# Attention probabilities of the first head turned by DMA and VectorE instead of TensorE

## The chip, the core and the metric

The kernel runs on one core of a Trainium2 chip. The metric is the device time of one launch, in microseconds. An execution of it is compared with executions of the kernel before on the same chip.

## What is computed

Sixteen sequences (B = 16) of 512 tokens with 512 features pass through three layers: linear attention with a small convolution (phase a), cross attention on a second sequence (phase b, which the change touches), and a gated recurrence over the sequences with an output layer (phases c and d). Cut to phase b, the reference is:

```python
NUM_HEADS, NUM_KV, HEAD_DIM, WIDTH = (4, 1, 128, 512)
xn = _rmsnorm(x, rms_scale)
mn = _rmsnorm(mem_seq, rms_scale)
q = jnp.einsum('BTD,NDH->BTNH', xn, q_w)
kv = jnp.einsum('BSD,cKDH->cBSKH', mn, kv_w)
k, v = (kv[0], kv[1])
q = _apply_rope(q, q_pos) * HEAD_DIM ** (-0.5)
k = _apply_rope(k, k_pos)
logits = jnp.einsum('BTKGH,BSKH->BKGTS', q, k, preferred_element_type=jnp.float32)
masked = jnp.where(mem_mask[:, None, None, None, :], logits, MASK_FILL)
probs = jax.nn.softmax(masked, axis=-1).astype(x.dtype)
enc = jnp.einsum('BKGTS,BSKH->BTKGH', probs, v).reshape(B, T, NUM_HEADS, HEAD_DIM)
return jnp.einsum('BTNH,NHD->BTD', enc, out_w)
```

## The kernel before

Every matrix is held as a high and a low part (`Split`), and `product` (L128 to L132) multiplies with three matmuls, high by high, high by low, low by high. Phase b is a software pipeline over the sequences (`pipeline3`): in one step the sequence `new` is prepared (keys, values, queries), `old` goes through the softmax, and `fin` gets its last encodings, the output product and the residual. There are 18 steps. A step has 16 slots (`j` from 0 to 15); each engine runs its own program, written by hand as a loop over the slots, strictly in that order. There is no scheduler: what an engine does in a slot is what the `if` lines say.

The softmax of one sequence has 16 tiles of 128 queries by 512 keys, four per head; tiles 0 to 3 are head 0. A tile passes through: `logits` on TensorE (two slots ahead of its own); `masked` on VectorE (L1531: mask, minimum and copy to one of four places of `soft`); `exp` on ScalarE (L1379); `one_over` on VectorE (L1520); `normalise` on GpSimd (L1316); `turn_p` on TensorE (L1723: four 128x128 transposes into PSUM, at the end of its slot); `p_high` on ScalarE (L1388) and `p_low` on VectorE (L1539), which split the turned tile. `masked` of a tile waits until `turn_p` has read the tile four before it in `soft`. `encode` multiplies the four turned tiles of a head with the values: head 0 in slot 8, head 1 in slot 11, head 2 in slots 13 to 15, head 3 in slot 1 of the next step.

In the same slots `new` is worked on. Its normalised tokens `x` are turned without TensorE: SyncE stores them to DRAM (`out` is used as scratch, L1118), loads them back with 32-row blocks exchanged (`load_shuffled`, L382, four DMAs), and VectorE transposes 32x32 squares within partitions (`tokens_turned`, L388, slots 5 to 8). ScalarE splits the result (`tokens_high`, slots 5 to 8, each ahead of that slot's `exp`), GpSimd makes the low part (`tokens_low`, L1320), and TensorE takes it in `queries(0)` in slot 9. `residual` (VectorE, slots 5 to 8) empties the banks of `out`, the output product of `fin` (TensorE, slots 4 to 7); `out`, keys, queries and `turn_keys` share three PSUM banks in turn, so that `out(3)` takes the bank that `residual(0)` has emptied and `turn_keys` the one of `residual(1)`.

All DMAs are issued by SyncE, one after the other, and SyncE stands still at each wait. Before, its order in a step is: load `res`; wait for the normalised tokens and store them; wait for the store and issue the four shuffled loads; load the mask, the next memory (L1109) and the next tokens; store the finished sequence.

## Time and profile before

| | |
|---|---|
| median of 3 runs | 3030.55 us (3030.36 to 5046.9) |
| profiled execution | 3028.35 us, of which the span of the instructions is 3026.6 us |
| TensorE busy | 2983.4 us (99%), 14628 matmuls |
| VectorE, ScalarE, GpSimd busy | 1952.0 us (64%), 1295.3 us (43%), 919.5 us (30%) |
| mean granted TensorE clock | 0.997 of full speed |
| the probabilities' transposes (L1723) | 1024, busy 154.5 us |
| one step of phase b | 57.3 us, from the token store at 1452.44 us to the next at 1509.66 us |

The time of an execution is 1.75 us more than its span, and the sums below are made against the profiled execution. A matmul's row overlaps the next one's, so that what a group costs TensorE is read from start to start. In the timelines a number in brackets is the idle time ahead of a row and what ended it.

### The profile page before, as it was taken

The page shows a single profiled execution, that of the slowest core. Times are in us where ns is not written, and L with a number is a line of the kernel's source. Part 1 is how long each engine was busy: PE and PEld are TensorE (multiplying, and loading weights), DVE is VectorE, ACT ScalarE, POOL GpSimd, SP SyncE. Part 2 cuts the span into 40 slices and gives each one's busy share as a digit, 9 for nine tenths or more (in the row PEclk, how much of TensorE's full clock was granted, in tenths as well). Part 3 has the DMA queues.
Part 4 walks back from the last instruction along what each step waited for, and adds up shares of the span by engine and source line. Part 5 has one row for each costly group of instructions (what it writes and reads, how often), then busy time and mean ns, then how long its engine had stood idle before and what let it go on. Part 6 is the DMA issues. An engine that isn't in the chain of part 4 may idle for free.

```text
span 3026.6 us, 39400 instructions
## 1 busy us (share of the span) xinstructions
PE 2983.4 (99%) x14628; PEld 2508.4 (83%) x14628; DVE 1952.0 (64%) x4095; ACT 1295.3 (43%) x2511; POOL 919.5 (30%) x681
## 2 busy tenths in 40 slices
PE   7999999999989999999999999999999999999999
PEld 6888888888868888888888878888888888888887
DVE  6888888888878888888888774323333433232455
ACT  4444444444457766767766643211112212112243
POOL 0101010101357877777777720000000000000144
PEclk9999999999999999999999999999999999999999
DMA  7777777777733334344344232111111121111486
GB/s 212 201 203 209 202 215 199 215 198 217 205 105 113 105 107 127 99 113 127 99 114 126 71 125 74 56 54 55 42 42 42 56 55 57 42 28 46 153 290 224
DMA packets 319631, 380.07 MB, mean 126 GB/s; under 512 B 15312, under 2 KB 175056, under 8 KB 319440
## 3 DMA queue, kind: packets, MB, share of 16 engines
q1 hardware_dynamic: 319440, 377.56, 43.2%
q8 instruction: 116, 1.90, 0.3%
q14 instruction: 75, 0.61, 0.1%
HBM read 232.80 MB, written 130.02 MB: 120 GB/s over the span
## 4 chain that ended last, share of the span: by engine, by line
PE 96%; DVE 2%; ACT 1%; issue 1%; DMA 0%; POOL 0%; SPq 0%; DVEq 0%; ACTq 0%; POOLq 0%
PE c_p L132 11%; PE c_p L131 11%; PE c_p L130 11%; PE a_p L130 6%; PE a_p L131 6%; PE a_p L132 6%; PE b_n L130 5%; PE b_n L132 5%; PE b_n L131 5%; PE b_t L1723 3%; PE d_p L131 2%; PE d_p L132 2%; PE d_p L130 2%; PE a_p L1017 2%; PE a_r L131 2%; PE a_r L132 2%
## 5 line engine op out<-in xcount | busy, mean ns | idle before, releaser
L1316 POOL TENSOR_SCALAR b_soft<-b_soft,b_one_in_sum 128x512 f32<-128x512 f32 x256 | 401.2, 1568 | 201.5 <-DVE b_one_in_sum L1520 201.3
L1997 ACT ACTIVATE c_gate<-c_p,c_bias 128x512 f32<-128x512 f32 x180 | 124.2, 690 | 682.6 <-PE c_p L132 682.6
L2027 DVE TENSOR_TENSOR c_gate<-c_gate,c_gate 128x512 f32<-128x512 f32 x64 | 44.2, 691 | 502.7 <-ACT c_gate L1997 502.7
L351 POOL TENSOR_TENSOR kept_scale<-c_ln_ve,minus_half 128x4 f32<-128x4 f32 x16 | 16.1, 1008 | 880.4 <-DVE c_ln_ve L343 880.4
L1531 DVE CUSTOM_DVE_ANT_0 b_soft<-b_l,b_mask_row 128x512 f32<-128x512 f32 x256 | 175.6, 686 | 87.9 <-issue 84.0
L351 POOL TENSOR_TENSOR a_ln_sc<-a_ln_ve,minus_half 128x4 f32<-128x4 f32 x16 | 16.3, 1017 | 629.9 <-DVE a_ln_ve L343 629.9
L1379 ACT ACTIVATE b_soft<-b_soft,b_minus_top 128x512 f32<-128x512 f32 x256 | 184.5, 721 | 44.6 <-DVE b_minus_top L1531 42.6
L649 ACT ACTIVATE a_elu<-a_p 128x512 f32<-128x512 f32 x128 | 75.6, 591 | 287.6 <-PE a_p L132 287.6
L1388 ACT ACTIVATE b_p_hi<-b_t 128x512 fp32r<-128x512 f32 x256 | 151.3, 591 | 109.9 <-PE b_t L1723 109.6
L1539 DVE TENSOR_TENSOR b_p_lo<-b_t,b_p_hi 128x512 fp32r<-128x512 f32 x256 | 175.7, 686 | 16.1 <-ACT b_p_hi L1388 14.3
L1723 PE MATMUL b_t<-ident,b_soft 128*128 128x128 f32 x1024 | 154.5, 273 | 4.9 <-POOL b_soft L1316 4.9
L2221 POOL TENSOR_TENSOR d_x<-d_x,d_y 128x512 f32<-128x512 f32 x60 | 79.8, 1332 | 252.8 <-ACT d_y L2238 252.8
L1723 PEld LDWEIGHTS b_t<-ident,b_soft 128*128 128x128 f32 x1024 | 126.0, 142 | 30.5 <-DVE b_p_lo L1539 6.4
L130 PE MATMUL b_l<-b_k_hi,b_q_hi 128*128 128x512 f32 x256 | 123.2, 481 | 2.0 <-POOL b_q_lo L1328 1.6
L2029 DVE TENSOR_TENSOR c_gate<-c_gate,c_c_f 128x512 f32<-128x512 f32 x64 | 44.3, 692 | 116.3 <-ACT c_gate L1997 116.3
L130 PE MATMUL a_p<-a_Wk_hi,a_xT_hi 128*128 128x512 f32 x256 | 105.3, 411 | 0.7 <-DVE a_Wk_lo L194 0.7
L626 POOL TENSOR_TENSOR a_res<-a_res,a_bp 128x512 f32<-128x512 f32 x64 | 82.3, 1318 | 75.9 <-DMA a_res<-in_x 47.4
L666 ACT ACTIVATE a_z_hi<-a_z_sum 128x512 fp32r<-128x512 f32 x64 | 40.5, 633 | 150.2 <-DVE a_z_sum L848 150.2
L130 PE MATMUL b_n<-b_nT_hi,b_qw_hi 128*128 128x512 f32 x256 | 100.7, 393 | 3.0 <-POOL b_nT_lo L1320 3.0
L130 PE MATMUL b_e<-b_p_hi,b_v_hi 128*128 128x512 f32 x256 | 100.4, 392 | 2.9 <-DVE b_enc_lo L1544 2.9
L132 PE MATMUL b_l<-b_k_hi,b_q_lo 128*128 128x512 f32 x256 | 102.0, 398 | 0.0
L130 PE MATMUL a_r<-a_Wp_hi,a_z_hi 128*128 128x512 f32 x256 | 101.2, 395 | 0.0
(301 smaller groups left out, 9617.6 us busy)
## 6 DMA issues: line engine op xcount, KB each, us to landing
a_mem_moving<-in_ctx SPq DMA_DIRECT2D x64, 256.0 KB, 5.2
a_mem_turned<-in_ctx SPq DMA_DIRECT2D x16, 1024.0 KB, 9.2
x<-a_mem_turned SPq DMA_DIRECT2D x16, 1024.0 KB, 7.8
a_res<-in_x SPq DMA_DIRECT2D x16, 1024.0 KB, 6.4
x<-a_res SPq DMA_DIRECT2D x16, 1024.0 KB, 5.2
b_memT_f<-x SPq DMA_DIRECT2D x16, 1024.0 KB, 7.3
b_x<-x SPq DMA_DIRECT2D x16, 1024.0 KB, 6.1
b_res<-x SPq DMA_DIRECT2D x16, 1024.0 KB, 5.5
```

Of the source, the lines that this page charges most:

```text
L130: pe.matmul(out, stationary.high, moving.high, start=first, stop=False)
L131: pe.matmul(out, stationary.high, moving.low, start=False, stop=False)
L132: return pe.matmul(out, stationary.low, moving.high, start=False, stop=last)
L626: pool.tensor_tensor(res[:, t, :], res[:, t, :], bp[:, :], ALU.add).then_inc(res_bp.sem, res_bp.unit)
L1316: pool.tensor_scalar(soft[:, at, :], soft[:, at, :], one_in_sum[:, at:at + 1], None, ALU.mult).then_inc(p_norm.sem, p_norm.unit)
L1379: act.activation(soft[:, at, :], soft[:, at, :], ACT.Exp, bias=minus_top[:, at:at + 1], scale=-1.0, accum_out=row_sum[:, at:at + 1]).then_ ...
L1388: act.activation(p[h % 2].high[:, :, t * P:(t + 1) * P], pT_banks[j % 2][:, :].rearrange("p (i s) -> p i s", i=T), ACT.Copy).then_inc(p_hi ...
L1531: dve.tensor_tensor_reduce(out=soft[:, at, :], in0=logit_banks[j % 2][:, :], in1=mask_row[b % 2][:, :], scale=-1.0, scalar=3e38, op0=ALU.a ...
L1539: dve.tensor_tensor(part.low, pT_banks[j % 2][:, :].rearrange("p (i s) -> p i s", i=T), part.high_f32(), ALU.subtract).then_inc(p_lo.sem, ...
L1723: mm = pe.transpose(pT_banks[j % 2][:, i * P:(i + 1) * P], soft[:, tile(old.b, j), i * P:(i + 1) * P], self.ident[:, :])
L1997: act.activation(gate[j % 2][i][:, :], gating.banks[(3 * j + i) % 6][:, :], ACT.Tanh if g == "c" else ACT.Sigmoid, bias=added[:, i, j:j + ...
L2221: pool.tensor_tensor(x[old.par][:, t, :], x[old.par][:, t, :], y[:, t % 2, :], ALU.add).then_inc(out_sb.sem, out_sb.unit)
```

## The change

In phase b the four tiles of head 0 are no longer turned by TensorE. For each, SyncE stores the normalised tile to DRAM (`store_p`, rows of `out`); for each half of two tiles it loads the blocks back exchanged, four DMAs of 64 KB for a tile (`load_p`, eight for a half), into the half of the second probability buffer that is free at that time, each tile with a place of its own (`shuffled_p`); VectorE transposes 32x32 squares (`first_head_turned`, slots 3 to 6); ScalarE and GpSimd split (`first_head_high`, `first_head_low`, slots 4 to 7). `load_p` of the second half also waits for the loads of the first. The place in `soft` of tiles 0 to 3 comes free when their stores have landed, in pairs (`soft_free`, `k | 1`). A square transpose yields columns that are interleaved by four, so the columns of keys and mask are written in that order (`by_column`, `by_tile`), and `turn_p` of heads 1 to 3 reads its columns with a step of four. Some semaphores are merged (`kvq_ps`, `k_mask`), with the same waits.

```diff
         SLOTS = 4
+        HEAD = 4
         with ExitStack() as held:
...
             q = self.split(ctx, "b_q", [P, H, S])
+            p0_at = self.place.offset
             p = [self.split(ctx, f"b_p{i}", [P, T, S]) for i in range(2)]
+            p0_raw = Place(nc, p0_at + 4 * T * S).tile("b_p0_raw", [P, T, S])
+            p1_raw = [Place(nc, p0_at + 4 * T * S * (2 + i)).tile(f"b_p1_raw{i}", [P, T, S]) for i in range(2)]
             memT = Split(sb("memT_hi", [P, C, S], F32R), Place(nc, self.base + 1024 * 196).tile("b_memT_lo", [P, C, S], F32R))
             memT_f = Place(nc, self.base + 1024 * 196).tile("b_memT_f", [P, C, S])
             rope = sb("rope", [P, 4, S])
...
-            def shuffle_x(sp, b):
+            def store_p(sp, b, t):
+                sp.wait_ge(p_norm.sem, p_norm.upto(b, t))
+                sp.dma_start(self.out[b, t * P:(t + 1) * P, :], soft[:, t, :]).then_inc(p_stored.sem, p_stored.unit)
+
+            def load_p(sp, b, half):
+
+                sp.wait_ge(p_stored.sem, p_stored.upto(b, 2 * half + 1))
+                if half == 1:
+                    sp.wait_ge(p_loaded.sem, p_loaded.upto(b, 7))
+                if half == 0 and b >= 1:
+                    sp.wait_ge(enc_ps.sem, enc_ps.upto(b - 1))
+                for i in range(2):
+                    t = 2 * half + i
+                    for a in range(4):
+                        sp.dma_start(shuffled_p(t)[32 * a:32 * (a + 1), :, :],
+                                     self.out[b, t * P:(t + 1) * P, a * P:(a + 1) * P].rearrange("(g m) n -> m g n", m=32)).then_inc(p_loaded.sem, p_loaded.unit)
+
+            def shuffled_p(t):
+                return p1_raw[t // 2][:, :, (2 + t % 2) * P:(3 + t % 2) * P]
+
+            def store_x(sp, b):
                 sp.wait_ge(N.normed.sem, N.normed.upto(b))
                 sp.dma_start(self.token_rows(self.out, b), x[:, :, :]).then_inc(x_moved.sem, x_moved.unit)
+
+            def shuffle_x(sp, b):
                 sp.wait_ge(x_moved.sem, x_moved.upto(b - 1, 0))
                 self.load_shuffled(sp, x, self.out, b, x_moved)
...
+            def by_tile(row):
+                return row[:, :].rearrange("p (i w) -> p w i", i=T)
+
+            def by_column(row):
+                return row[:, :].rearrange("p (w i) -> p w i", i=T)
+
+            def soft_free(b, j):
+
+                g = b * J + j - SLOTS
+                if g < 0:
+                    return None
+                item, k = divmod(g, J)
+                if k < T:
+                    return p_stored.sem, p_stored.upto(item, k | 1)
+                return pT_ps.sem, pT_ps.upto(item, k - T)
+
...
                             sp.wait_ge(self.a_stored.sem, self.a_stored.upto(B - 1))
                         sp.dma_start(res[:, :, :], self.token_rows(self.x1, fin.b)).then_inc(res_in.sem, res_in.unit)
+                    if old:
+                        store_p(sp, old.b, 0)
+                    if new and new.b >= 1:
+                        store_x(sp, new.b)
+                    if old:
+                        store_p(sp, old.b, 1)
+                        load_p(sp, old.b, 0)
                     if new and new.b >= 1:
                         shuffle_x(sp, new.b)
+                    if old:
+                        store_p(sp, old.b, 2)
+                        store_p(sp, old.b, 3)
+                        load_p(sp, old.b, 1)
                     if following(new, B):
...
+                    def first_head_low(t):
+                        pool.wait_ge(p_hi.sem, p_hi.upto(old.b, high_at[t]))
+                        part = (slice(None), slice(None), slice(t * P, (t + 1) * P))
+                        pool.tensor_tensor(p[0].low[part], p0_raw[part], p[0].high[part].bitcast(F32), ALU.subtract).then_inc(p0_lo.sem, p0_lo.unit)
+
...
-                        act.wait_ge(pT_ps.sem, pT_ps.upto(b, j))
+                        act.wait_ge(pT_ps.sem, pT_ps.upto(b, j - T))
+                        if j == T + 2:
+                            act.wait_ge(p_lo.sem, p_lo.upto(b, first_turned_at[T - 1]))
...
+                    def first_head_high(t):
+                        act.wait_ge(p_lo.sem, p_lo.upto(old.b, first_turned_at[t]))
+                        part = (slice(None), slice(None), slice(t * P, (t + 1) * P))
+                        act.activation(p[0].high[part], p0_raw[part], ACT.Copy).then_inc(p_hi.sem, p_hi.unit)
...
-                        act.activation(k[new.par].high[:, :], turns.bank(s, KT)[:, :], ACT.Copy).then_inc(k_hi.sem, k_hi.unit)
+                        act.activation(by_column(k[new.par].high), by_tile(turns.bank(s, KT)), ACT.Copy).then_inc(k_hi.sem, k_hi.unit)
...
-                        if old and j >= 1:
+                        if old and j >= T + 1:
                             p_high(old.b, j - 1)
+                        if old and HEAD <= j < HEAD + T:
+                            first_head_high(j - HEAD)
...
-                        if free := earlier(pT_ps, b, j, SLOTS):
+                        if free := soft_free(b, j):
...
+                    def first_head_turned(t):
+                        dve.wait_ge(p_loaded.sem, p_loaded.upto(old.b, 8 * (t // 2) + 7))
+                        if t == 0 and old.b >= 1:
+                            dve.wait_ge(enc_ps.sem, enc_ps.upto(old.b - 1, 2))
+                        blocks = shuffled_p(t).rearrange("p g (n i) -> p i g n", i=T)
+                        dve.transpose(p0_raw[:, :, t * P:(t + 1) * P].rearrange("p i (g n) -> p i g n", g=T), blocks).then_inc(p_lo.sem, p_lo.unit)
...
-                        dve.tensor_tensor(k[new.par].low[:, :], turns.bank(s, KT)[:, :], k[new.par][:, :].high_f32(), ALU.subtract).then_inc(k_lo.sem, k_lo.unit)
+                        dve.tensor_tensor(by_column(k[new.par].low), by_tile(turns.bank(s, KT)), by_column(k[new.par].high.bitcast(F32)), ALU.subtract).then_inc(k_mask.sem, k_mask.unit)
...
-                        dve.tensor_scalar(mask_row[new.par][:, :], mask_u8[new.par][:, :], -1.0, BIG, ALU.add, ALU.mult).then_inc(mask_f.sem, mask_f.unit)
+                        dve.tensor_scalar(by_column(mask_row[new.par]), by_tile(mask_u8[new.par]), -1.0, BIG, ALU.add, ALU.mult).then_inc(k_mask.sem, k_mask.unit)
...
-                        if old and j >= 1:
+                        if old and j >= T + 1:
                             p_low(old.b, j - 1)
+                        if old and HEAD - 1 <= j < HEAD - 1 + T:
+                            first_head_turned(j - HEAD + 1)
...
-                        if free := earlier(p_lo, old.b, j, 2):
-                            pe.wait_ge(*free)
+                        if j >= T + 2:
+                            pe.wait_ge(p_lo.sem, p_lo.upto(old.b, low_at[j - 2]))
+                        elif old.b >= 1:
+                            pe.wait_ge(p_lo.sem, p_lo.upto(old.b - 1, low_at[J - 2 - T + j]))
                         pe.wait_ge(p_norm.sem, p_norm.upto(old.b, j))
                         for i in range(T):
-                            mm = pe.transpose(pT_banks[j % 2][:, i * P:(i + 1) * P], soft[:, tile(old.b, j), i * P:(i + 1) * P], self.ident[:, :])
+                            mm = pe.transpose(pT_banks[j % 2][:, i * P:(i + 1) * P], interleaved(soft[:, tile(old.b, j), :], i, T), self.ident[:, :])
...
-                            pe.wait_ge(p_lo.sem, p_lo.upto(item.b, h * T + T - 1))
+                            if h == 0:
+                                pe.wait_ge(p0_lo.sem, p0_lo.upto(item.b))
+                            else:
+                                pe.wait_ge(p_lo.sem, p_lo.upto(item.b, low_at[h * T + T - 1]))
...
-                        if old:
+                        if old and j >= T:
                             turn_p(j)
```

SyncE's program for one step, before (rows L1279 to L1114 are one step; `b_x<-out` are the shuffled loads of the tokens):

```order
L1279 DMA b_res<-x 128x4x512 [waits b_stored]
L1118 DMA out<-b_x 128x4x512 [waits b_ln_normed]
L382 DMA b_x<-out 32x16x128 [waits b_x_moved]
L382 DMA b_x<-out 32x16x128 x3
L1127 DMA b_mask_u_212<-in_mask_BxS_bk 128x512 [waits b_mask_f,b_mask_in]
L1109 DMA b_memT_f<-x 128x4x512 [waits b_kv_ps]
L1114 DMA b_x<-x 128x4x512 [waits b_x_turned]
```

The same stretch now (`out<-b_soft` are the stores of head 0's tiles, `b_p_raw` the places of their loads, `b_p_stored` and `b_p_loaded` their landings):

```order
L1324 DMA b_res<-x 128x4x512 [waits b_stored]
L1125 DMA out<-b_soft 128x512 [waits b_p_norm]
L1145 DMA out<-b_x 128x4x512 [waits b_ln_normed]
L1125 DMA out<-b_soft 128x512 [waits b_p_norm]
L1137 DMA b_p_raw_189<-out 32x4x128 [waits b_enc_ps,b_p_stored]
L1137 DMA b_p_raw_189<-out 32x4x128 x7
L382 DMA b_x<-out 32x16x128 [waits b_x_moved]
L382 DMA b_x<-out 32x16x128 x3
L1125 DMA out<-b_soft 128x512 [waits b_p_norm] x2
L1137 DMA b_p_raw_190<-out 32x4x128 [waits b_p_loaded,b_p_stored]
L1137 DMA b_p_raw_190<-out 32x4x128 x7
L1156 DMA b_mask_u_216<-in_mask_BxS_bk 128x512 [waits b_k_mask,b_mask_in]
```

Twenty DMAs have come in; the shuffled loads of the tokens stand behind the first half's loads, and the mask and the next memory behind the second half's.

VectorE's program in slot 5, before, from `one_over(6)` to `residual(0)` (the MEMSET and the two ISA rows are `masked`):

```order
L1520 RECIPROCAL b_one_in_sum<-b_row_sum 128x1 [waits b_p_exp]
L1530 MEMSET b_carrier 128x1 [waits b_pT_ps,b_logit_ps]
L1531 ISA b_soft,b_minus_top<-b_l,b_mask_row_214 128x512
L1531 ISA b_minus_top 128x1
L1539 TENSOR_TENSOR b_p_lo<-b_t,b_p_hi 128x4x128 [waits b_p_hi]
L388 STREAM_TRANSPOSE b_nT_f<-b_x 128x512 [waits b_q_ps,b_x_moved]
L1550 TENSOR_TENSOR b_res<-b_n,b_res 128x512 [waits b_out_ps,b_res_in]
```

And now:

```order
L1592 RECIPROCAL b_one_in_sum<-b_row_sum 128x1 [waits b_p_exp]
L1602 MEMSET b_carrier 128x1 [waits b_p_stored,b_logit_ps]
L1603 ISA b_soft,b_minus_top<-b_l,b_mask_row_217 128x512
L1603 ISA b_minus_top 128x1
L1611 TENSOR_TENSOR b_p_lo<-b_t,b_p_hi 128x4x128 [waits b_p_hi]
L1619 STREAM_TRANSPOSE b_p_raw<-b_p_raw_190 128x4x128 [waits b_p_loaded]
L388 STREAM_TRANSPOSE b_nT_f<-b_x 128x512 [waits b_kvq_ps,b_x_moved]
L1629 TENSOR_TENSOR b_res<-b_n,b_res 128x512 [waits b_out_ps,b_res_in]
```

`masked` (of tile 7 here, and of tile 6 in slot 4) waits for stores to land, and the transpose of the tokens stands behind a transpose that waits for the second half's loads.

## Rows read from the trace of the kernel before

The slot borders of this step on TensorE are the starts of the `b_l` matmuls that follow each group of transposes.

**Rows 1.** The page: the chain that ended last, by engine.

```profile
PE 96%; DVE 2%; ACT 1%; issue 1%; DMA 0%; POOL 0%; SPq 0%; DVEq 0%; ACTq 0%; POOLq 0%
```

**Rows 2.** Attention phase: engines busy (us, instructions), granted clock, DMA share, GB/s.

```profile
940.00:2100.00 1160.00, 1153.33 (x5939) 972.98 (x5938) 824.00 (x2098) 654.50 (x1356) 648.85 (x466) 1.00 0.33 98
```

**Rows 3.** TensorE's timeline, one step: start and length in us.

```profile
1450.98 0.60 PE L1723 MATMUL b_t<-ident,b_soft 128*128 128x128 f32 x4
1451.33 0.48 PE L130 MATMUL b_l<-b_k_hi,b_q_hi 128*128 128x512 f32 x1
...
1468.09 0.47 PE L130 MATMUL b_l<-b_k_hi,b_q_hi 128*128 128x512 f32 x1
...
1477.04 0.40 PE L130 MATMUL b_e<-b_p_hi,b_v_hi 128*128 128x512 f32 x1
```

**Rows 4.** TensorE's timeline: a group of interleaved transposes.

```profile
851.20 0.64 PE L369 MATMUL b_n<-ident,b_x 128*128 128x128 f32 x4
851.59 0.48 PE L130 MATMUL a_r<-a_Wp_hi,a_z_hi 128*128 128x512 f32 x1
```

**Rows 5.** Weight loads of interleaved transposes: ns min/median/max, first, last start.

```profile
L369 PEld LDWEIGHTS b_n<-ident,b_x x16: 196/210/221, 847.8 to 857.9; 128*128 128x128 f32 x16
```

**Rows 6.** Weight loads of the probabilities' transposes, same columns.

```profile
L1723 PEld LDWEIGHTS b_t<-ident,b_soft x1024: 137/140/230, 880.3 to 1785.7; 128*128 128x128 f32 x171
```

**Rows 7.** SyncE's timeline of DMA issues, one step.

```profile
1452.44 0.38 SPq L1118 DMA_DIRECT2D out<-b_x  x1
1456.76 1.93 SPq L382 DMA_DIRECT2D b_x<-out  x4
1458.80 0.59 SPq L1127 DMA_DIRECT2D b_mask_u<-in_mask_BxS_bk  x1
```

**Rows 8.** All DMA issues: count, KB each, median us to landing.

```profile
b_memT_f<-x SPq DMA_DIRECT2D x16, 1024.0 KB, 7.3
...
out<-b_x SPq DMA_DIRECT2D x15, 1024.0 KB, 4.3
...
c_x_shuffled<-c_x SPq DMA_DIRECT2D x224, 64.0 KB, 2.1
...
out<-d_x SPq DMA_DIRECT2D x4, 256.0 KB, 2.0
```

**Rows 9.** DMA issues of 1458.6 to 1459.5 us alone.

```profile
b_x<-out SPq DMA_DIRECT2D x1, 256.0 KB, 6.2
b_mask_u<-in_mask_BxS_bk SPq DMA_DIRECT2D x1, 64.0 KB, 5.8
```

**Rows 10.** SyncE's time per 32x4x128 issue: ns min/median/max.

```profile
L376 SPq DMA_DIRECT2D c_x_shuffled<-c_x x224: 591/601/1754, 1860.3 to 2691.9; - x112
```

**Rows 11.** GpSimd's timeline, one step.

```profile
1454.72 1.56 POOL L1316 TENSOR_SCALAR b_soft<-b_soft,b_one_in_sum 128x512 f32<-128x512 f32 x1 [0.32 <-DVE b_one_in_sum L1520]
...
1470.71 1.30 POOL L1320 TENSOR_TENSOR b_nT_lo<-b_nT_f,b_nT_hi 128x512 fp32r<-128x512 f32 x1
```

**Rows 12.** VectorE's timeline, one step.

```profile
1462.21 0.69 DVE L1531 CUSTOM_DVE_ANT_0 b_soft<-b_l,b_mask_row 128x512 f32<-128x512 f32 x1
...
1466.43 1.08 DVE L388 STREAM_TRANSPOSE b_nT_f<-b_x 128x512 f32<-128x512 f32 x1
...
1470.29 1.09 DVE L388 STREAM_TRANSPOSE b_nT_f<-b_x 128x512 f32<-128x512 f32 x1
```

**Rows 13.** ScalarE's timeline, one step.

```profile
1467.55 0.64 ACT L1416 ACTIVATE b_nT_hi<-b_nT_f 128x512 fp32r<-128x512 f32 x1 [2.47 <-DVE b_nT_f L388]
1468.09 0.71 ACT L1379 ACTIVATE b_soft<-b_soft,b_minus_top 128x512 f32<-128x512 f32 x1
...
1472.65 0.62 ACT L1243 ACTIVATE b_memT_hi<-b_memT_f 128x512 fp32r<-128x512 f32 x1
```

**Rows 14.** Engines busy and granted clock around two of TensorE's waits.

```profile
889.00:891.00 2.00, 0.62 (x3) 0.18 (x1) 2.00 (x7) 0.60 (x1) 1.54 (x2) 1.00 1.26 188
893.00:895.00 2.00, 1.02 (x4) 0.47 (x3) 1.98 (x4) 0.00 (x0) 1.41 (x1) 0.50 1.05 388
```

More of the change, by code:

```diff
@@ L1233, in phase_b @@
             jobs = [(k_rope, 2, 0), (k_rope, 6, 0)] + [(x2_sb, t, 2) for t in range(T)]
-            jobs += [(k_lo, 0, 0)] + [(q_cos, h, 0) for h in range(H)]
+            jobs += [(k_mask, 0, 0)] + [(q_cos, h, 0) for h in range(H)]
             pT_banks = self.banks(held, "b_t", 2)
@@ L1336, in step @@
                             normalise(new.b, 0)
+                        if old and HEAD <= j < HEAD + T:
+                            first_head_low(j - HEAD)
                         if older_goes_on:
@@ L1397, in values_high @@
                     def values_high(g):
-                        act.wait_ge(kv_ps.sem, kv_ps.upto(new.b, g))
+                        act.wait_ge(kvq_ps.sem, kvq_ps.upto(new.b, g))
                         if g == 0 and new.b >= 2:
@@ L1440, in step @@
                     for j in range(J):
-                        if old and j >= 1:
+                        if old and j >= T + 1:
                             p_high(old.b, j - 1)
+                        if old and HEAD <= j < HEAD + T:
+                            first_head_high(j - HEAD)
                         if fin:
```

41 lines of the change are left out of this document (22 added, 19 removed).

## The prediction

> **What bounds the kernel now.** I read the chain of waits first: 96% of it is TensorE's own work [rows 1]. The table of busy time for the attention phase says the same of the stretch that the change touches: TensorE is busy 1153 of 1160 us, while VectorE has 824, ScalarE 655 and GpSimd 649, at full granted clock [rows 2]. So TensorE work taken out pays in full only while nobody makes TensorE wait, and each microsecond of a new wait costs a microsecond of a step. The timelines of the single engines over one step then give both the prices and, more important here, the clock times at which things are ready. I use the step that stores its tokens at 1452.44 us [rows 7].
>
> **What TensorE saves.** A group of four transposes takes 0.35 us from its start to the next matmul, and that next matmul is 0.08 us longer than the usual 0.40 us [rows 3]: about 0.44 us a group with it. Four groups in each of 16 sequences: 64 x 0.44 = 28.2 us. The other 192 groups now read columns with a step of four. Such a group of tokens takes 0.39 us to the next matmul [rows 4] against 0.35: 192 x 0.035 = 6.7 us dearer. The single weight load, though, takes 210 ns with the step against 140 ns without [rows 5, 6].
>
> The Trainium skill, SBUF — State Buffer, Door 1: The DMA port swizzle, states that each access that crosses to a new 16-byte line pays a penalty, which is this step; and Perfetto Trace Analysis, Identifying the Most-Contended Engine, wants TensorE judged by the busy share of its weight loads. By these rules the price would be 192 x 4 x 0.07 = 54 us, more than the saving, and a perfectly hidden trip would end at 3054 us. The start-to-start times are what TensorE pays in this trace, and I go by them.
>
> On their own these two terms make -21.5 us, 0.7%.
>
> **What the others get.** VectorE swaps a `p_low` for a square transpose of 1.08 us [rows 12], at most 0.4 us more each, 1.6 us a step; GpSimd gets four subtractions of 1.30 us [rows 11], 5.2 us a step; both have over 15 us of room in a step of 57.3 us. ScalarE's work stays. Keys and mask are written with a step once a sequence; between nothing and the double of 0.6 us, and nobody waits there, so I take nothing. What is not covered is the time of the trip itself.
>
> **The trip, followed in time.** All times are on the clock of the step before the change.
>
> 1. The tokens' store is issued at 1452.44 us and lands 4.3 us later, when the shuffled loads begin, 1456.76 [rows 7, 8]. Tile 1's store stands behind it. 1024 KB take 4.3 us and 256 KB 2.0 us [rows 8], so another 256 KB cost 0.77 us: it lands at 1457.5.
> 2. Only then SyncE issues the eight loads of the first half. The same form, 32x4x128, takes it 0.60 us each in the recurrence [rows 10]: 4.8 us, to 1462.3. VectorE wants this half in slot 3, and already waits there.
> 3. The tokens' shuffled loads now begin at 1462.3 instead of 1456.76. They took 1.93 us to issue, and the last landed 6.2 us after its own issue [rows 7, 9], 7.6 us after the first issue: now 1469.9.
> 4. The stores of tiles 2 and 3 have been ready for long (GpSimd starts on tile 3 at 1454.72, 1.56 us [rows 11]) but are issued at 1464.2 to 1465.0, behind 1 MB. The mask, 64 KB behind the same loads, landed 5.8 us after its issue at 1458.80, just behind them [rows 7, 9]; so I let the stores land behind the loads too: 1469.9 + 2 x 0.77 = 1471.4.
> 5. `masked(6)` on VectorE waits for that, in slot 4; before it ran at 1462.21 [rows 12]. It ends at 1472.1. TensorE's next product, `logits(8)`, began at 1468.09 [rows 3], and would be ready for it 1.8 us sooner: the saving of the four groups is swallowed here. Behind `masked(6)` also stand the second half of the keys' work and `residual`, whose banks TensorE needs for the output product.
> 6. The second half's loads: 1471.4 + 4.8 = 1476.2, the last one issued at 1475.6 and landed 2.1 us later [rows 8]: 1477.7. VectorE waits for it in slot 5, ahead of the tokens' own transpose.
> 7. From here a ring of VectorE and ScalarE sets the pace, not TensorE: tokens' transpose, `tokens_high` 1.12 us after its start, `exp` 0.54 us later [rows 12, 13], then `one_over`, `masked`, `p_low`, the next tokens' transpose. Before, one round took 1470.29 - 1466.43 = 3.86 us [rows 12], a slot's length, without idle time to give. Now: head 0's third transpose 1477.7 to 1478.8, tokens 0 at 1478.8, one round and the fourth head transpose 3.86 + 1.08: tokens 1 at 1483.7. `tokens_high(1)` at 1484.8, `exp` at 1485.4 for 0.71, the memory's high part 0.62, `p_high(6)` about as much, head 0's last high part 0.64 [rows 13]: 1488.0. GpSimd's low part of it 1.30 [rows 11]: 1489.3. The memory load, moved behind all this, is issued near 1476.8 and lands 7.3 us later [rows 8], 1484.1, in time for 1486.1.
> 8. `encode(0)` waits for that low part. Before it started at 1477.04 [rows 3]: 12.3 us later. `queries(0)`, next on TensorE, gets the tokens' last low parts about then. Later slots have no new wait.
>
> So a step with both an old and a new sequence loses 12.3 us; there are 15: 184.5 us. Of the dearer groups, eight of twelve lie behind slot 8 and count: 15 x 8 x 0.035 = 4.2 us. The sixteenth sequence has no tokens beside it; without them stores 2 and 3 go out by 1460 and I give that step its saving, 1.8 us.
>
> **The clock.** Where TensorE stood still at the phase's start (busy 0.62 of 2 us), the granted clock fell from 1.00 to 0.50, 2.4 to 1.2 GHz, and stayed there two microseconds later [rows 14]. Here TensorE idles over a third of slots 4 to 7. Most work at the low clock hides in the waits; what follows them does not. `encode(0)`, twelve matmuls of about 0.23 us from start to start, can cost 2.8 us more. Between nothing and that I take half, 1.4 us: 21 us in all.
>
> **Sum.** 3028.35 + 184.5 + 4.2 - 1.8 + 21 = 3236 us, against the profiled execution of 3028.35 us; the median of the runs, 3030.55 us, is 2.2 us above that, which changes nothing here. A measurement tells about 2% from no change: below 2970 or above 3091 us.
>
> **Rivals.**
>
> *The trip is late, but less.* If stores do not queue behind earlier DMAs and an issue costs 0.48 us as in the tokens' loads [rows 7]: tile 1 lands with the tokens at 1456.7, first half issued to 1460.6, tokens to 1462.5, store 3 lands 2.0 us [rows 8] after 1463.0, second half's last load issued at 1468.4 and landed at 1470.5. The ring from there ends 7.2 us earlier: 5.1 us a step, 76.5 us, 3107 us with the small terms and no clock. Against it stands the mask, which queued. The Trainium skill, DMA: Bandwidth & Descriptors, Anatomy of one DMA, gives a DMA 2.0 us plus its bytes over 436 GB/s with no word of what is ahead of it, for GpSimd's queue. By this rule each store lands 2.6 us after its issue; the trace agrees for the lone token store (4.4 by it, 4.3 measured) and not behind a queue. 18%.
>
> *The trip is hidden, not slower.* TensorE arrives at `encode(0)` at 1475.3 (1477.04 less the saving). The ring needs 11.6 us from the second half's landing to there, so the half must be there by 1463.7. Tile 3 is ready at 1456.3; with 2.0 us for the store, eight issues of 0.48 us and 2.1 us for the last, 1463.7 is reached only with nothing else in SyncE's program. It decides whether SyncE gets to tile 3 by then, and the order of its issues says no. If so: 3028.35 - 28.2 + 6.7 = 3007 us, no change by measure. 8%.
>
> *The waits feed on each other.* If the clock stays low over `encode(0)` and the two query products behind it (from 1477.04 to about 1487.5), or issues slow down to their longest [rows 10], a step loses about 5 us beside the 12.3: 3028 + 184.5 + 2.4 + 75 = 3290 us. 16%.
>
> My forecast keeps 58%.
>
> **Numbers.** 3236 us. The range runs from 3092 to 3320 us: it holds the forecast, most of the late-but-less case and the slow one. Slower by over 2%: 0.90 (forecast, slow case, most of the second); within 2%: 0.09; faster 0.01, since the whole saving is below 1%.
>
> **What would show it.** In the profile after: waits of VectorE for DMA at `masked` and at the new transpose of some microseconds, 15 times each; TensorE busy well below 99% in the phase and a step of about 70 us; a start of head 0's `encode` some 37 us after the token store instead of 24.6; SyncE's second-half loads issued 19 us after it; the clock at 0.50 in slots 4 to 8. The transposes' groups would be 192 with 0.39 us each. I am wrong if stores land 2 us after their issue behind the tokens' loads, if eight loads are issued in much less than 4.8 us, or if the ring can run faster than 3.86 us a round.

## The result, and the profile after

The changed kernel takes 3200.5 us (median of four runs, 3199.16 to 3202.7), the kernel before 3030.45 us: ratio 1.0566, 95% interval 1.0553 to 1.058, slower. Of the executions one of the kernel before took 5046.9 us, and one of the third experiment 6725.5; the ratios leave both out. The forecast was 3236 us in a range of 3092 to 3320. The profiled execution took 3199.18 us, 170.8 us more than that of before. Of this the steps with an old and a new sequence hold nearly all: from one token store to the next it is 68.16 us (mean of 11 steps, 952.08 to 1701.87 us) against 57.23 (937.32 to 1681.31), 10.9 us a step and 164 us in 15.

The page's chain of waits, by engine, and the attention phase (engines busy, instructions, granted clock, DMA share, GB/s), against [rows 1, 2]:

```profile
PE 78%; DMA 6%; SPq 4%; ACT 4%; DVE 4%; issue 2%; POOL 2%; DVEq 0%; POOLq 0%; ACTq 0%
```

```profile
940.00:2100.00 1160.00, 1037.22 (x5029) 857.51 (x5029) 789.98 (x2026) 629.79 (x1326) 734.60 (x533) 0.96 0.40 119
```

TensorE's share of the chain went from 96% to 78%, DMA and SyncE's queue came in with 10%, and TensorE stands still in 123 of 1160 us where it stood in 7. One step on SyncE's timeline, against [rows 7] (start, length in us; the places of the program are those of the order shown with the change):

```profile
1497.50 0.38 SPq L1145 DMA_DIRECT2D out<-b_x  x1
1497.93 0.51 SPq L1125 DMA_DIRECT2D out<-b_soft  x1
1502.46 3.68 SPq L1137 DMA_DIRECT2D b_p_raw<-out  x8
1506.18 2.03 SPq L382 DMA_DIRECT2D b_x<-out  x4
1508.25 0.96 SPq L1125 DMA_DIRECT2D out<-b_soft  x2
1514.86 3.66 SPq L1137 DMA_DIRECT2D b_p_raw<-out  x8
1518.62 0.38 SPq L1156 DMA_DIRECT2D b_mask_u<-in_mask_BxS_bk  x1
```

VectorE in the same step; the bracket is the idle time before an instruction and what ended it ([rows 12] before). The two MEMSETs open `masked(4)` and `masked(6)`:

```profile
1502.57 0.06 DVE L1602 MEMSET b_carrier<- 128x1 f32 x1 [3.34 <-DMA out<-b_soft]
...
1507.71 1.10 DVE L1619 STREAM_TRANSPOSE b_p_raw<-b_p_raw 128x512 f32<-128x512 f32 x1 [2.67 <-DMA b_p_raw<-out]
...
1514.97 0.06 DVE L1602 MEMSET b_carrier<- 128x1 f32 x1 [4.39 <-DMA out<-b_soft]
...
1520.06 1.11 DVE L1619 STREAM_TRANSPOSE b_p_raw<-b_p_raw 128x512 f32<-128x512 f32 x1 [0.37 <-DMA b_p_raw<-out]
1521.10 1.06 DVE L388 STREAM_TRANSPOSE b_nT_f<-b_x 128x512 f32<-128x512 f32 x1
...
1525.95 1.07 DVE L388 STREAM_TRANSPOSE b_nT_f<-b_x 128x512 f32<-128x512 f32 x1
```

Four waits for the trip, 10.8 us in this step, and then a round of 4.85 us between the tokens' transposes (1521.10 to 1525.95) where it was 3.86. Behind these rounds TensorE begins the first head's encode:

```profile
1531.63 0.47 PE L130 MATMUL b_e<-b_p_hi,b_v_hi 128*128 128x512 f32 x1 [2.15 <-POOL b_p_lo L1381]
1531.94 0.47 PE L131 MATMUL b_e<-b_p_lo,b_v_hi 128*128 128x512 f32 x1
1532.21 0.63 PE L132 MATMUL b_e<-b_p_hi,b_v_lo 128*128 128x512 f32 x1
1532.63 0.63 PE L130 MATMUL b_e<-b_p_hi,b_v_hi 128*128 128x512 f32 x1
```

That is 34.1 us after the token store, where it was 24.6 [rows 3, 7]; over the twelve whole steps from 952.08 to 1771.17 us it is 34.8 in the mean (34.1 to 36.1). The matmuls behind it start 0.43 us apart instead of 0.23: from 1531.60 to 1535.60 us the granted clock is 0.57. The granted clock ahead of the encode in the next step, which has the same order (its tokens are stored at 1566.04, its `encode(0)` starts at 1601.55), against [rows 14]:

```profile
1586.00:1590.00 4.00, 2.72 (x8) 1.90 (x7) 3.59 (x13) 1.43 (x4) 1.54 (x2) 0.59 0.44 128
1590.00:1594.00 4.00, 4.00 (x13) 3.12 (x13) 3.17 (x6) 1.89 (x5) 1.53 (x3) 0.56 0.81 240
1594.00:1598.00 4.00, 3.82 (x19) 2.89 (x18) 3.50 (x6) 1.49 (x3) 3.82 (x3) 1.00 0.09 35
```

Here the clock fell to the lower level, 1.2 GHz, and was back at 2.4 GHz in the window that begins 7.6 us before `encode(0)`: it stretched an output product whose end had to wait anyway, and from VectorE's third turned tile to `encode(0)` it is 11.6 us in this step as in the one before. But in the step shown first the clock fell once more, behind TensorE's wait of 2.15 us, over `encode(0)` itself. Its twelve matmuls took 4.42 us there and 2.83 us in the next step. That is so in 7 of the 15 steps (about 4.4 us in each), and a step with it is longer by 1.6 us from `encode(0)` to the next token store (34.4 against 32.8): 11 us in all. Twelve whole steps are longer than before by 11.0 us in the mean: 10.2 by the late encode, 0.7 by the clock over it (five of the twelve), and 0.2 behind it.

### The profile page after: what moved, and what is told of

It is laid out like the page before. It is cut to its first block, busy times and chain, and to the rows that moved or that the text cites. A ratio compares the mean times of both kernels' runs of the same rounds, so it can differ in the third digit from the quotient of the medians.

```text
span 3197.3 us, 39255 instructions
## 1 busy us (share of the span) xinstructions
PE 3025.4 (95%) x14372; PEld 2523.3 (79%) x14372; DVE 1965.5 (61%) x4095; ACT 1294.2 (40%) x2511; POOL 1001.3 (31%) x745
## 4 chain that ended last, share of the span: by engine, by line
PE 78%; DMA 6%; SPq 4%; ACT 4%; DVE 4%; issue 2%; POOL 2%; DVEq 0%; POOLq 0%; ACTq 0%
PE c_p L131 11%; PE c_p L130 11%; PE c_p L132 11%; PE a_p L130 5%; PE a_p L132 5%; PE a_p L131 5%; DMA out<-b_soft 5%; SPq L1137 3%; PE b_n L130 2%; PE b_n L131 2%; PE b_n L132 2%; PE d_p L130 2%; PE d_p L131 2%; PE d_p L132 2%; PE a_r L132 2%
## 5 line engine op out<-in xcount | busy, mean ns | idle before, releaser
L130 PE MATMUL b_n<-b_ow_hi,b_enc_hi 128*128 128x512 f32 x256 | 114.3, 446 | 38.5 <-DVE b_k_swap L1659 37.2
L1453 ACT ACTIVATE b_p_hi<-b_t 128x512 fp32r<-128x512 f32 x192 | 112.8, 588 | 80.3 <-PE b_t L1806 78.9
L130 PE MATMUL b_e<-b_p_hi,b_v_hi 128*128 128x512 f32 x256 | 107.5, 420 | 37.7 <-POOL b_p_lo L1381 34.5
L1611 DVE TENSOR_TENSOR b_p_lo<-b_t,b_p_hi 128x512 fp32r<-128x512 f32 x192 | 131.9, 687 | 10.4 <-ACT b_p_hi L1453 9.7
L1806 PE MATMUL b_t<-ident,b_soft 128*128 128x128 f32 x768 | 124.9, 286 | 11.5 <-POOL b_soft L1372 11.5
L131 PE MATMUL b_n<-b_ow_lo,b_enc_hi 128*128 128x512 f32 x256 | 109.4, 427 | 0.0
L132 PE MATMUL b_n<-b_ow_hi,b_enc_lo 128*128 128x512 f32 x256 | 108.9, 425 | 0.0
L131 PE MATMUL b_e<-b_p_lo,b_v_hi 128*128 128x512 f32 x256 | 104.9, 410 | 0.0
```

The source lines that it names most:

```text
L130: pe.matmul(out, stationary.high, moving.high, start=first, stop=False)
L131: pe.matmul(out, stationary.high, moving.low, start=False, stop=False)
L132: return pe.matmul(out, stationary.low, moving.high, start=False, stop=last)
L1453: act.activation(p[h % 2].high[:, :, t * P:(t + 1) * P], pT_banks[j % 2][:, :].rearrange("p (i s) -> p i s", i=T), ACT.Copy).then_inc(p_hi ...
L1611: dve.tensor_tensor(part.low, pT_banks[j % 2][:, :].rearrange("p (i s) -> p i s", i=T), part.high_f32(), ALU.subtract).then_inc(p_lo.sem, ...
L1806: mm = pe.transpose(pT_banks[j % 2][:, i * P:(i + 1) * P], interleaved(soft[:, tile(old.b, j), :], i, T), self.ident[:, :])
```

## The experiments

The theory ahead of the runs: the whole loss is the waits for the trip (landing of stores behind the tokens' loads, SyncE's issue time, landing of loads), and without them the change would give 20 us. Rivals: the columns with a step of four, which cost 54 us if every longer weight load is paid in full; and that the loss is in the engines' own work.

**The columns alone.** Before, with keys, mask and all 256 groups interleaved, no trip:

```diff
-mm = pe.transpose(pT_banks[j % 2][:, i * P:(i + 1) * P], soft[:, tile(old.b, j), i * P:(i + 1) * P], self.ident[:, :])
+mm = pe.transpose(pT_banks[j % 2][:, i * P:(i + 1) * P], interleaved(soft[:, tile(old.b, j), :], i, T), self.ident[:, :])
```

> The kernel before with the interleaved columns alone: keys and mask are written by column, and all 256 groups of TensorE's transposes read with a step of four; no trip through DRAM. By start-to-start times (0.39 against 0.355 us a group) it costs 256 x 0.035 = 9 us: about 3039 us, no change by measure. The rival, the rule that goes by the time of the weight loads (210 against 140 ns), gives 256 x 4 x 0.07 = 72 us: about 3100 us.

Measured: 3039.74 against 3031.23 us, 1.0027 [1.0016, 1.0039]; 8.5 us for 256 groups, 0.033 us a group (by the interval 5 to 12 us in all). The single weight load did take 1.5 times as long in the changed kernel, min/median/max in ns, against [rows 6]:

```profile
L1806 PEld LDWEIGHTS b_t<-ident,b_soft x768: 195/210/231, 892.1 to 1956.4; 128*128 128x128 f32 x192
```

Four loads are 0.28 us longer in a group, and 0.033 us of that was paid; the rest lay beside other work. The time from start to start was the price.

**No trip.** The changed kernel without the stores and loads; nothing waits for a store any more, and VectorE's transposes read other data of the same shape, so head 0's probabilities are not what is computed:

```diff
-dve.wait_ge(p_loaded.sem, p_loaded.upto(old.b, 8 * (t // 2) + 7))
+dve.wait_ge(p_norm.sem, p_norm.upto(old.b, t))
+dve.wait_ge(q_hi.sem, q_hi.upto(old.b, 0))
...
-blocks = shuffled_p(t).rearrange("p g (n i) -> p i g n", i=T)
+blocks = q.high[:, 0, :].bitcast(F32).rearrange("p (g n i) -> p i g n", g=T, i=T)
```

> The changed kernel without the stores and loads of head 0's probabilities: VectorE's four transposes read a part of the queries that lies in SBUF, so head 0's result is not the attention's, and no place of the probabilities waits for a store. All work of the engines is as in the change. My theory, that the loss is the waits for the trip, gives a step near 57 us: 28 us saved, 7 us for the stride, and 0 to 1 us a step because two transposes of 1.08 us now stand in the ring of VectorE and ScalarE ahead of encode(0): 3010 to 3045 us. The rival, that the added work on VectorE and GpSimd makes the loss, keeps it near 3200 us.

Measured: 3061.91 us, 1.0099 [1.0084, 1.0114]. The trip's waits are 139 of 170 us. But nothing of the saving came: 31 us are lost with no trip at all, a miss of the 3010 to 3045 us expected. TensorE's waits from 940 to 1900 us (total, times, longest):

```profile
PE b_e L130 <- POOL b_p_lo L1372: 30.1, 14, 2.2
```

Behind five of these 14 waits `encode(0)` ran at the lower clock, 4.2 to 4.4 us instead of 2.8: 7 us of the 31.

**Stores 2 and 3 ahead of the loads.** SyncE waits for the landing of store 1, then stores tiles 2 and 3, then loads:

```diff
-                sp.wait_ge(p_stored.sem, p_stored.upto(b, 2 * half + 1))
...
+                        sp.wait_ge(p_stored.sem, p_stored.upto(old.b, 1))
+                        store_p(sp, old.b, 2)
+                        store_p(sp, old.b, 3)
```

> The changed kernel with one move in SyncE's program: the stores of tiles 2 and 3 go out as soon as tile 1's has landed, ahead of the first half's loads and of the tokens' shuffled loads. If the loss is the order on SyncE and the queue (my theory), masked(6) no longer waits, the second half's loads are issued about 12 us after the tokens' store instead of 17.4, and land behind the tokens near 17; some 5 us a step less: 3125 us, between 3105 and 3145. If the amount of traffic is what delays everything, or if the wait only changes its place, it stays at 3185 us or more.

Measured: 3157.58 us, 1.0411 [1.0394, 1.0429]: 43 us better than the change, a miss, 33 us above the middle of the range expected and 13 above its upper end. `masked(6)` waits no more; VectorE's waits for DMA in one step are now

```profile
1472.49 0.06 DVE L1603 MEMSET b_carrier<- 128x1 f32 x1 [3.38 <-DMA out<-b_soft]
...
1478.64 1.08 DVE L1620 STREAM_TRANSPOSE b_p_raw<-b_p_raw 128x512 f32<-128x512 f32 x1 [3.69 <-DMA b_p_raw<-out]
...
1487.43 1.10 DVE L1620 STREAM_TRANSPOSE b_p_raw<-b_p_raw 128x512 f32<-128x512 f32 x1 [0.59 <-DMA b_p_raw<-out]
```

The third transpose came 20.0 us after the token store instead of 22.6. The second half's loads went out 11.9 us after it instead of 17.4, but now they queued behind the tokens' loads and landed 5 us or more after their issue (2.0 us in the changed kernel, where the queue was empty by then).

**Issues doubled.** Each 64 KB load as two of 32 KB, same bytes:

```diff
...
+for part in range(2):
+    g = slice(2 * part, 2 * part + 2)
+    sp.dma_start(shuffled_p(t)[32 * a:32 * (a + 1), g, :], rows[:, g, :]).then_inc(p_loaded.sem, p_loaded.unit)
```

> The changed kernel with each of the 64 KB loads cut into two of 32 KB: the same bytes and packets, 32 issues a sequence on SyncE instead of 16. If the issue time is a term of the chain (my theory; 0.46 us each in the changed kernel), each half takes 3.7 us more and both lie on the chain: 7.3 us a step, 110 us, about 3310 us. If only the landing counts, it costs under 1 us a step: 3200 to 3215 us.

Measured: 3311.5 us, 1.0919 [1.0903, 1.0935]: 111 us for 16 more issues a sequence. SyncE in one step:

```profile
1491.69 7.54 SPq L1140 DMA_DIRECT2D b_p_raw<-out  x16
...
1507.76 7.40 SPq L1140 DMA_DIRECT2D b_p_raw<-out  x16
```

Two blocks of 7.5 us where they were 3.7: 7.6 us a step, or 114 in 15, as expected. SyncE's issue time is on the chain in full.

**The 31 us: the order inside a slot.** Two moves: VectorE turns the first head's tile behind `residual` instead of ahead of the tokens' tile, and GpSimd makes its low part ahead of its normalisation. First on the kernel without a trip:

```diff
+                        if old and HEAD <= j < HEAD + T:
+                            first_head_low(j - HEAD)
                         if old and j < J - 1:
                             normalise(old.b, j + 1)
...
                         if fin and sums <= j < sums + T:
                             residual(j - sums)
+                        if old and HEAD - 1 <= j < HEAD - 1 + T:
+                            first_head_turned(j - HEAD + 1)
```

> The kernel without the trip (its transposes read a part of the queries, as in the run before) with two moves inside the slots: VectorE's transpose of head 0 comes after residual, where it falls into the 0.83 us in which VectorE waits for exp, and GpSimd's subtraction comes ahead of normalise. If the 33 us that the version without the trip lies above the kernel before come from the ring of VectorE and ScalarE (my theory), a round gets 0.8 us shorter, encode(0) waits under 1 us instead of 2.15, and it ends at 3015 to 3030 us, below the kernel before. If they come from elsewhere (GpSimd's and VectorE's share of the memory, more work in all), it stays at 3050 to 3062 us.

Measured: 3055.81 us, 1.0080 [1.0065, 1.0096]: 6 us better, and inside what the rival gave. The wait ahead of `encode(0)` was halved (14.5 us in 14 steps instead of 30.1) and the encode ran at the full clock in all of them, but two new waits for GpSimd came, 10.7 us together. That the memory slows the engines, which is part of the rival, is not seen: GpSimd's instructions take 1.56 and 1.30 us and VectorE's transposes 1.1, as before. On the changed kernel itself, with its late trip:

> The changed kernel with the two moves inside the slots alone, the trip as late as in the change. The trip's landing sets the chain and the ring only its last stretch: two rounds shorter by 0.8 us at most, 1.6 us a step, 24 us: 3170 to 3190 us. If the ring were the main cause, it would come to 3100 us or less.

Measured: 3159.21 us, 1.0424 [1.0408, 1.0439]: 41 us better than the change and 11 below the range expected. Some 8 us of the gain are the clock's, which was low over one encode from 940 to 1900 us instead of six. The order counts more where the trip is late, and is worth 6 us where there is none.

**An early trip.** The turned tiles' source gets the place of head 0's high parts, so that the loads wait for the encode of head 2 and not of head 3, and SyncE stores tiles 0 and 1 ahead of the tokens, and tiles 2 and 3 ahead of the tokens' loads:

```diff
-                    sp.wait_ge(enc_ps.sem, enc_ps.upto(b - 1))
+                    sp.wait_ge(enc_ps.sem, enc_ps.upto(b - 1, 2))
...
-                return p1_raw[t // 2][:, :, (2 + t % 2) * P:(3 + t % 2) * P]
+                return p0_shuffled[:, :, t * P:(t + 1) * P]
```

> The changed kernel with the trip taken as early as its data allow. The shuffled probabilities go into the first buffer's own high half instead of the second buffer, so that the loads wait for head 2 of the sequence before and not for head 3; SyncE's order is stores 0 and 1, the tokens' store, loads of the first half, stores 2 and 3, the tokens' shuffled loads, loads of the second half. Counted from the tokens' store: first half landed at 6, stores 2 and 3 at 7, tokens at 12.5, second half at 13.5 us instead of 22.6, before VectorE wants it much. My theory: the waits for the trip go, and what the ring costs stays: 3062 to 3080 us, as without the trip. The rival, that the traffic of the trip costs by itself wherever it stands, gives over 3120 us.

Measured: 3118.74 us, 1.0291 [1.0276, 1.0307], between the two figures and at the rival's end. The trip was not hidden yet: VectorE waited for its loads 29 times from 940 to 1900 us, 54.6 us in all. With the two moves inside the slots on top:

> The early trip with the two moves inside the slots (VectorE's transpose behind residual, GpSimd's subtraction ahead of normalise). Its result is the reference's. If both parts of the loss are understood, it lands with the version that has no trip and the same two moves, or up to 15 us above it: 3020 to 3040 us, the first with the trip that is no slower than the kernel before. If the two do not add, 3060 us or more.

Measured: 3059.74 us, 1.0095 [1.0079, 1.0112], 4 us from the kernel without a trip, and 20 above the range expected. VectorE's waits for the loads are down to 4.3 us. So the trip can be hidden but for some 4 us, and 29 us of loss stay. The hidden trip of the second rival is there, and it is not 3007 us.

**What is left.** TensorE's timeline of the kernel without a trip and with both moves (line numbers of that kernel), the groups of transposes and the waits of slots 5 to 9:

```profile
1484.21 0.64 PE L1798 MATMUL b_t<-ident,b_soft 128*128 128x128 f32 x4
...
1488.76 0.72 PE L1798 MATMUL b_t<-ident,b_soft 128*128 128x128 f32 x4 [0.48 <-POOL b_soft L1363]
...
1493.20 0.65 PE L1798 MATMUL b_t<-ident,b_soft 128*128 128x128 f32 x4
...
1495.60 0.47 PE L130 MATMUL b_e<-b_p_hi,b_v_hi 128*128 128x512 f32 x1 [1.05 <-POOL b_p_lo L1372]
...
1498.45 0.64 PE L1798 MATMUL b_t<-ident,b_soft 128*128 128x128 f32 x4
...
1502.35 0.50 PE L130 MATMUL b_n<-b_nT_hi,b_qw_hi 128*128 128x512 f32 x1 [0.28 <-POOL b_nT_lo L1367]
...
1503.15 0.64 PE L1798 MATMUL b_t<-ident,b_soft 128*128 128x128 f32 x4
...
1507.07 0.64 PE L1798 MATMUL b_t<-ident,b_soft 128*128 128x128 f32 x4
```

A slot without a wait is 3.92 us (1503.15 to 1507.07). The three with one are 4.55, 5.25 and 4.70: 2.7 us longer, of which the brackets show 1.81. The rest is that the bracket counts from the modelled end of the last matmul (0.39 us long, started every 0.23), and that the first ones after a wait are longer. All three waits are for GpSimd, whose instructions at that time are these:

```profile
1489.78 1.30 POOL L1372 TENSOR_TENSOR b_p_lo<-b_p_raw,b_p_hi 128x512 fp32r<-128x512 f32 x1 [1.16 <-ACT b_p_hi L1450]
1491.06 1.56 POOL L1363 TENSOR_SCALAR b_soft<-b_soft,b_one_in_sum 128x512 f32<-128x512 f32 x1
1492.59 1.29 POOL L1367 TENSOR_TENSOR b_nT_lo<-b_nT_f,b_nT_hi 128x512 fp32r<-128x512 f32 x1
1494.17 1.28 POOL L1372 TENSOR_TENSOR b_p_lo<-b_p_raw,b_p_hi 128x512 fp32r<-128x512 f32 x1 [0.29 <-ACT b_p_hi L1450]
```

4.15 us of work in slots of 3.9. Four repairs follow, all with the early trip and both moves. The second and the third stand on the first, the fourth on the third. In the first ScalarE normalises tiles 6, 7, 8 (0.71 us there):

```diff
+act.activation(soft[:, at, :], soft[:, at, :], ACT.Copy, scale=one_in_sum[:, at:at + 1]).then_inc(p_norm.sem, p_norm.unit)
```

> The early trip with both in-slot moves (3059.74 us), and ScalarE instead of GpSimd normalises tiles 6, 7 and 8 (0.6 us there against 1.57 us). Theory: what is left over the kernel before is GpSimd, which in slots 6 and 7 of a step now has a low part of the first head (1.29 us), a normalisation (1.57) and a low part of the tokens (1.29), 4.15 us in slots of 3.9 us; TensorE waits for it at three places of each step (0.48, 1.05 and 0.28 us idle in the kernel without a trip, and 2.9 us longer slots there in all). Two of the three places go, and the wait ahead of the first encode shrinks but stays, because it hangs on the low part of tile 3 behind ScalarE's queue: 3030 to 3042 us. Rival: the residue is TensorE's own (strided columns, restarts), or VectorE's full round of 3.9 us: then it stays within 5 us of 3059.7.

Measured: 3055.37 us, 1.0087 [1.0074, 1.0101], a miss: against 1.0095 [1.0079, 1.0112] no gain that is clear of noise, so that GpSimd's load alone was not the cause. Two of the three waits did go, and the third took their place (it was 17.4 us with the early trip and both moves):

```profile
PE b_e L130 <- POOL b_p_lo L1382: 25.8, 14, 1.9
```

Second: VectorE takes the tokens' tile behind `residual` too, and behind the first head's tile; ScalarE makes tile 3's high part ahead of head 1's:

```diff
+                        if old and j == HEAD + T - 1:
+                            first_head_high(T - 1)
                         if old and j >= T + 1:
                             p_high(old.b, j - 1)
```

> As the kernel with ScalarE's normalisations, and VectorE turns the first head's tile ahead of the tokens' tile, ScalarE makes the high part of tile 3 ahead of head 1's. Tile 3's low part should end about 1.1 us earlier, at about the moment at which TensorE reaches the first encode. Theory of GpSimd and queue order: 3015 to 3030 us, so faster than the kernel before (3030.6), by the 1.48 us of TensorE time saved a step less the stride. Rival: the wait moves to the tokens' products or to the third turned tile's load (0.57 us wait in the early trip), and it stays at or above 3035 us.

Measured: 3134.87 us, 1.0348 [1.0334, 1.0362], the worst miss: 80 us slower than the first. `tokens_high` stands ahead of `exp` on ScalarE, so a late tokens' tile makes the exponential late and VectorE waits for its sums, in every slot (VectorE's waits, total and times, this kernel and then the first repair):

```profile
DVE b_one_in_sum L1605 <- ACT b_soft L1446: 87.4, 88, 1.4
```

```profile
DVE b_one_in_sum L1602 <- ACT b_soft L1445: 32.3, 61, 1.4
```

TensorE then waited 4.0 us ahead of each `encode(0)` instead of 1.8, and all 14 encodes from 940 to 1900 us ran at the lower clock (4.1 to 5.3 us), where with the first repair three did. That alone is some 23 of the 80 us.

Third, from the first: only tile 3, in slot 6, and `exp` ahead of `tokens_high` there (the next memory's first high part goes to slot 7):

```diff
+                        if old and j == 6:
+                            first_head_high(T - 1)
+                            if new:
+                                tokens_high(j - first)
```

> The kernel in which ScalarE normalises tiles 6 to 8 (3055.37 us), whose TensorE has one wait a step left (1.83 us before the first encode, for the low part of tile 3), with tile 3 taken earlier in one slot alone: in slot 6 VectorE turns it ahead of the tokens' tile, ScalarE makes its high part in slot 6 behind the exponential and ahead of the tokens' high part, and the memory's first high part goes to slot 7. The exponential no longer stands behind the tokens' high part there, which is what I take to have ruined the kernel that moved all tokens' tiles (VectorE waited 87 us for the exponential's sums there). Theory (GpSimd's load, then queue order, are all that is left): tile 3's low part ends 1.5 to 2 us earlier, a step loses the wait and the restart of 0.3 us behind it, about 2.1 us x 15 = 32 us: 3018 to 3032 us, at or below the kernel before. Rival: another input is as late (the tokens' low parts, the third turned tile's load), and it stays at 3040 us or above.

Measured: 3052.15 us, 1.0073 [1.0059, 1.0086], where the rival had it, and with the interval of the first repair again no gain clear of noise. The wait ahead of the encode went to 0.5 us a step, and another input was late. TensorE's waits, and GpSimd at that place in one step:

```profile
PE b_n L130 <- POOL b_nT_lo L1378: 19.6, 28, 0.9
PE b_e L130 <- POOL b_p_lo L1383: 7.0, 14, 1.2
```

```profile
1438.05 1.57 POOL L1374 TENSOR_SCALAR b_soft<-b_soft,b_one_in_sum 128x512 f32<-128x512 f32 x1 [2.38 <-DVE b_one_in_sum L1609]
1439.58 1.28 POOL L1378 TENSOR_TENSOR b_nT_lo<-b_nT_f,b_nT_hi 128x512 fp32r<-128x512 f32 x1
```

GpSimd sat idle for 2.38 us in front of a normalisation, with the tokens' low part behind it. Fourth: tile 9 to ScalarE too, `exp` first in slot 7, the last tokens' tile turned ahead of `p_low` in slot 8:

```diff
-            by_scalar = (6, 7, 8)
+            by_scalar = (6, 7, 8, 9)
...
+                        if new and new.b >= 1 and j == 8:
+                            tokens_turned(3)
                         if old and j >= T + 1:
                             p_low(old.b, j - 1)
```

> The kernel that takes tile 3 first (3052.15 us) removed the wait before the first encode (0.16 us left) and got two others for it: TensorE idles 0.81 and 0.61 us before the third and fourth products with the tokens' low parts, since GpSimd ran a normalisation (1.57 us) after 2.4 us without work and ahead of them, and the tokens' high part stood ahead of an exponential. Here ScalarE normalises tile 9 too, the exponential of slot 7 goes ahead of the tokens' high part, and VectorE turns the last tokens' tile of slot 8 ahead of its low part. Theory (queue order on full helpers, one late input after the other): the two waits with their restarts, up to 1.9 us a step or 28 us, shrink to 0.3 us or less: 3024 to 3036 us. Rival: each repair makes the next input late, since VectorE's slots are full (3.9 us of work in a slot of 3.9): 3045 to 3055 us.

Measured: **3026.41 us** against 3030.23, 0.9988 [0.9979, 0.9997] (11 and 15 runs): as expected, and the one version that beats the kernel before, by 4 us, or 0.1%; its interval just leaves out no change. TensorE's wait and its busy time (944.8 of 960 us, where the first repair has 926.6):

```profile
PE b_e L130 <- POOL b_p_lo L1383: 8.7, 14, 1.3
```

```profile
940.00:1900.00 960.00, 944.80 (x4831) 799.98 (x4831) 790.16 (x1987) 653.91 (x1360) 632.13 (x464) 1.00 0.48 141
```

## Why the prediction was right, and where it was off

*TensorE's terms.* The stride (6.7 us for 192 groups) held: 8.5 us for 256. The saving of 28.2 us was there as TensorE time but reached the measured time only in the last experiment, and there in part.

*Steps 1 and 2.* Tile 1 landed by 1502.46, 4.96 us after the token store (forecast 5.1). The eight issues took 3.68 us, 0.46 each, not 0.60: the issue in the recurrence that gave the price has the same form, but copies within SBUF and not from DRAM. That is 1.1 us early at each half.

*A wait that the steps left out.* `masked(4)` reuses the places of tiles 0 and 1 and waits for their stores in slot 2: 3.34 us in the step shown. It cost nothing of its own, since VectorE stood still again behind it, for 4.39 us at `masked(6)`; with stores 2 and 3 ahead it was the first of three waits.

*Steps 3 to 6.* Tokens' loads began at +8.7 us (forecast 9.9), stores 2 and 3 landed and let the second half go at +17.4 (19.0), VectorE's third transpose ran at +22.6 (25.3). They are early mainly by the issue time, 1.1 us at the first and 2.2 at the last. That the stores queue behind the megabyte of loads is shown: 6.6 us from the issue at 1508.25 to the loads that wait for them, where the token store alone takes 4.4. The late-but-less rival had the issue price nearly right (0.48 us) and failed here.

*Steps 7 and 8.* The ring ran at 4.85 us with a head transpose in it (forecast 4.94) and 4.1 without. From the second half's landing to `encode(0)` the forecast had 11.6 us, and 11.6 were measured from the third turned tile. `encode(0)` came at +34.1 us in the step shown and at +34.8 in the mean (36.9). So it was late by 10.2 us a step (12.3): 153 us in 15 steps instead of 184.5. The mechanism was right; the term was too large by 2.1 us a step, about what 16 issues at 0.46 instead of 0.60 us are early (2.2 us).

*The clock*, 21 us, was mis-sized too. It fell as forecast in slots 4 to 7, where their end was a wait and it cost nothing, and over `encode(0)` in 7 of 15 steps, 1.6 us each: 11 us. The half of 2.8 us that the forecast took for every step was a choice, and about half of that was paid in the mean. The two terms are too large by 31.5 and 10 us, more than the 35.5 us by which the forecast was too high; some 4 us outside these steps, where the forecast had a saving of 1.8, go the other way and were not traced.

*What failed outright* bore on the rival with the hidden trip: the four subtractions of 1.30 us on GpSimd and the transposes on VectorE were put at nothing, because both engines "have over 15 us of room in a step of 57.3 us". The room is a mean over a step. In slots 6 and 7 GpSimd had none left, VectorE's slots were as full (3.9 us from turn to turn), and each input that was mended left the next one late; which is why the rival with a hidden trip was priced at 3007 us and the chip gave 3059.74. Its mechanism was possible; a saving of 21.5 us was forecast for it and a loss of 29 measured.

What stays open: the last version still lies 19 us above the 3007 us that the terms of the two edits make. The wait of 0.6 us a step before the encode, with the 0.3 us that a wait cost beyond its idle time, is by estimate some 14 us of that in 15 steps; the rest was not traced.

## What to carry over

Follow a round trip through DRAM issue by issue on the queue's own timeline: the issue time of every descriptor and the bytes ahead of a store on its queue counted here more than the bytes of the trip. Room on a helper engine has to be read per slot, at the place where the work lands: with four subtractions of 1.3 us moved onto an engine with 30% load, and the order of the others unchanged, 31 us were lost here with no trip at all, 7 of them by the lower clock behind the waits. And when a wait is removed on full engines, look for the input that is next late before counting the gain: it took three repairs that stand on each other, and a fourth that made things worse, to turn 3060 us into 3026.

## What the runs showed of the hardware

- Weight loads with a column step of four took 210 ns instead of 140, but a group of four cost 0.033 us more. The Trainium skill, SBUF — State Buffer, Door 1: The DMA port swizzle, puts a penalty, without a figure, on each access that crosses to a new 16-byte line. The 210 ns agree in direction; they are no price for the kernel.
- A wait cost TensorE about 0.3 us more than its idle time in the profile (2.7 us of longer slots for 1.81 us of waits in three places).
- The granted clock was at the lower level over the first head's encode in 7 of 15 steps of the changed kernel, where TensorE had stood still for 2.15 us ahead of it (3.7 us in the first step); in none of 14 behind 1.05 us, without a trip and with both moves; and in all 14 behind 4.0 us, in the second repair.
- A 256 KB store took 2.0 us alone [rows 8] and some 6 us behind 1 MB of loads. By the Trainium skill, DMA: Bandwidth & Descriptors, Anatomy of one DMA, whose fit of 2.0 us and the bytes over 436 GB/s is for GpSimd's queue, an estimate for it is 2.6 us, and that section has no term for what is ahead.
- The same 128x512 scaling took 0.71 us on ScalarE and 1.57 us on GpSimd.
